# Attention heads: the two engines that subtract take strict turns, and two small jobs of a head move

## The reference, cut to what matters

```python
helical = jnp.einsum('bhpsc,bhptc->bhst', qn, kn) / p
dot = jnp.einsum('bshd,bthd->bhst', qh, kh) / math.sqrt(hd)
attn = jax.nn.softmax(alpha * dot + (1.0 - alpha) * helical, axis=-1)
vh = v.reshape(b, s, h, hd)
out = jnp.einsum('bhst,bthd->bshd', attn, vh).reshape(b, s, e)
```

## Time and profile before

| what | us |
|---|---|
| median of 3 runs (5803.75 to 5820.13) | 5806.87 |
| the profiled execution: its own time | 5804.25 |
| its span in the profile | 5802.5 |
| VectorE busy in the span | 4611.0 |
| TensorE busy | 3469.0 |
| ScalarE busy | 3017.1 |
| GpSimd busy | 2940.2 |

### The profile page before, as it was taken

One profiled execution on the slowest core, in us unless ns is written; L12 is line 12 of the kernel. 1 busy time (PEld: TensorE's weight loads), 2 busy tenths in 40 slices (PEclk: granted clock), 3 DMA queues, 4 the chain that ended last, 5 costly groups with the idle time before them and its releaser, 6 DMA issues. The chain is left out here.

```text
span 5802.5 us, 67231 instructions
## 1 busy us (share of the span) xinstructions
PE 3469.0 (60%) x14472; PEld 1229.5 (21%) x14472; DVE 4611.0 (79%) x8081; ACT 3017.1 (52%) x3827; POOL 2940.2 (51%) x2350
## 2 busy tenths in 40 slices
PE   8972000000000004878865799999999999999668
PEld 3330000000000002333411133333333333333123
DVE  5464686999999996553677799999999999999452
ACT  5563000001000013552287398989898989899632
POOL 1002465777777772112055266666666666666512
PEclk9986555555555557989987699999999999999888
DMA  1016415232322222000123311111111111110210
GB/s 40 15 36 112 74 16 111 58 65 49 65 53 61 64 50 62 13 11 0 68 101 121 65 32 32 43 36 32 32 33 32 32 32 32 33 44 6 78 27 29
DMA packets 143836, 275.46 MB, mean 47 GB/s; under 512 B 73808, under 2 KB 87504, under 8 KB 136336
## 3 DMA queue, kind: packets, MB, share of 16 engines
q1 hardware_dynamic: 142128, 263.57, 19.3%
q10 hardware_dynamic: 1440, 8.65, 0.4%
HBM read 178.65 MB, written 93.36 MB: 47 GB/s over the span
## 5 line engine op out<-in xcount | busy, mean ns | idle before, releaser
L994 POOL TENSOR_TENSOR att_heads_rest<-att_heads_probs,att_heads_high 128x576 f16<-128x576 f32 x1024 | 1390.4, 1358 | 848.8 <-ACT att_heads_high L1081 843.4
L1111 DVE TENSOR_REDUCE att_heads_maxima<-att_heads_peek 128x1 f32<-128x512 f32 x2048 | 1309.8, 679 | 91.8 <-PE att_heads_peek L1007 67.7
L1079 ACT ACTIVATE att_heads_probs<-att_heads_scores 128x1024 f32<-128x1024 f32 x1024 | 1074.4, 1049 | 252.3 <-PE att_heads_scores L1025 245.3
L1025 PE MATMUL att_heads_scores<-att_heads_q,att_heads_k 128*128 128x512 f16 (+1 forms) x4096 | 1067.2, 382 | 32.3 <-issue 21.5
L1081 ACT ACTIVATE att_heads_high<-att_heads_scores 128x1024 f16<-128x1024 f32 x1024 | 1075.8, 1051 | 0.0
L1849 PE MATMUL delta_out_sums<-delta_out_squares,main_head_sum 128*128 128x512 f32 x32 | 17.7, 688 | 1761.0 <-ACT delta_out_squares L1878 1761.0
L1131 DVE TENSOR_TENSOR att_heads_rest<-att_heads_probs,att_heads_high 128x448 f16<-128x448 f32 x1024 | 901.5, 881 | 63.8 <-POOL att_heads_rest L994 44.5
L1007 PE MATMUL att_heads_peek<-att_heads_k,att_heads_q 112*128 112x512 f16 x2048 | 688.9, 396 | 98.4 <-DVE att_heads_maxima L1111 49.3
L1728 ACT ACTIVATE delta_scan_s_terms<-delta_scan_state,delta_scan_record 128x64 f32<-128x64 f32 x256 | 104.7, 409 | 1160.2 <-DVE delta_scan_state L1785 1160.2
L1025 PEld LDWEIGHTS att_heads_scores<-att_heads_q,att_heads_k 128*128 128x128 f16 (+1 forms) x4096 | 395.5, 98 | 452.7 <-issue 37.2
L1041 PE MATMUL att_heads_out<-att_heads_high,att_heads_v_head 128*64 128x512 f16 x2048 | 418.5, 405 | 6.2 <-DVE att_heads_rest L1131 4.7
(11 more groups left out here) (225 smaller groups left out, 5393.9 us busy)
## 6 DMA issues: line engine op xcount, KB each, us to landing
delta_scan_record<-delta_record SPq DMA_DIRECT2D x64, 1026.0 KB, 10.6
att_heads_q<-att_hel SPq DMA_DIRECT2D x192, 128.0 KB, 3.1
att_heads_k<-att_hel SPq DMA_DIRECT2D x192, 128.0 KB, 3.2
delta_record<-delta_chunks_record SPq DMA_DIRECT2D x64, 256.5 KB, 4.7
att_hel<-att_hel_high SPq DMA_DIRECT2D x32, 512.0 KB, 3.8
att_hel<-att_hel_rest SPq DMA_DIRECT2D x32, 512.0 KB, 4.3
att_o<-att_heads_out_copy SPq DMA_DIRECT2D x256, 32.0 KB
att_out_parts<-att_o ACTq DMA_DIRECT2D x8, 1024.0 KB, 13.6
```

The costliest lines, as they stand in the source:

```text
L994: nc.gpsimd.tensor_tensor(rest[:, step % 4, SPLIT:], probs[:, step % 4, SPLIT:], high[:, step % 4, SPLIT:], ALU.subtract).then_inc(rest_b_ ...
L1025: mm = nc.tensor.matmul(scores[:, step % 2, tokens(j)], k[0:rows, slot, number, tile * P:(tile + 1) * P], q[0:rows, slot, number, tokens(h ...
L1079: nc.scalar.activation(probs[:, step % 4], scores[:, step % 2], ACT.Exp, scale=LOGIT_SCALE).then_inc(probs_ready, 1)
L1111: nc.vector.tensor_reduce(maxima[:, m:m + 1], peek[:, m % 2], AX.X, ALU.max).then_inc(peek_read, 1)
```

## The change

GpSimd waits, before its subtraction of a step, for VectorE's of the step before as well. VectorE's share of the columns goes from 448 to 480, GpSimd's from 576 to 544. `BEFORE_COPY` goes from 2 to 5. `LAST_PEEKS` goes from 23 to 22, so that `shifts` runs one step earlier while the transposition stays at step 24, and `shift_rows` goes from step 25, ahead of that step's maxima, to step 24, behind them.

```diff
-        BEFORE_COPY = 2
+        BEFORE_COPY = 5
         PEEKS = QT * 4
-        LAST_PEEKS = 23
+        LAST_PEEKS = 22
         EARLY = PEEKS - 2 * (LAST_PEEKS + 1)
-        TURN_AT = LAST_PEEKS + 1
-        ROWS_AT = TURN_AT + 1
+        TURN_AT = LAST_PEEKS + 2
         LOADS = 18 * 16
-        SPLIT = 448
+        SPLIT = 480
...
-            return 2, range(2 * (step - TURN_AT), 2 * (step - TURN_AT) + 2)
+            return 2, range(2 * (step - LAST_PEEKS - 1), 2 * (step - LAST_PEEKS - 1) + 2)
...
                             pool.wait_ge(high_ready, head * STEPS + step + 1 + H_CREDIT)
+                            pool.wait_ge(rest_a_ready, head * STEPS + step + R_CREDIT)
                             nc.gpsimd.tensor_tensor(rest[:, step % 4, SPLIT:], probs[:, step % 4, SPLIT:], high[:, step % 4, SPLIT:],
                                                     ALU.subtract).then_inc(rest_b_ready, 1)
...
                         by, numbers = peeks_at(step)
-                        if step == ROWS_AT and exists(last, slot, 1):
-                            shift_rows(*later(quad, slot, 1))
                         if exists(last, slot, by):
                             read_peeks(*later(quad, slot, by), numbers)
+                        if step == TURN_AT and exists(last, slot, 1):
+                            shift_rows(*later(quad, slot, 1))
                         if step == LAST_PEEKS and exists(last, slot, 1):
                             shifts(*later(quad, slot, 1))
```

## The result

| | us |
|---|---|
| before, median of 10 runs (5803.75 to 5820.13) | 5810.09 |
| with the change, median of 10 runs (5825.05 to 5844.25) | 5836.27 |
| ratio, with its 95% interval | 1.0041 (1.0032 to 1.0050) |
| span of the profiled execution with the change | 5835.6 |

The change makes the kernel 26 us slower, and the interval leaves out no change.

What follows compares the result with a forecast made beforehand. GpSimd's and VectorE's alternating subtractions were taken to bound every step of the heads' stage: 1023 x 2.115 us plus extras gave 2209.8 against 2185.3, +24.5 us, so 5830 in all, range 5786 to 5865.

Steps and rivals of the forecast that it cites:

- The four terms: Each step: GpSimd's subtraction, handing to VectorE, VectorE's subtraction, handing back, in series; 2.115 us.
- GpSimd's start behind VectorE: Fourth term, from VectorE's end to GpSimd's start: 0.14 us, with 0.09 as the lower end.
- the rival: Short handing over from VectorE to GpSimd, if a satisfied first semaphore costs nothing: 0.09 us, about 5779; 15 in 100.
- the copy: GpSimd's copy of values between two subtractions, once a head: ends 0.33 us late, 10.2 us in all.
- The turn of the loop: TensorE issues nothing for 3.65 us, 7 times; 4.9 us each reach the chain, 34.3 in all.
- The two more maxima: Two more maxima before the first step: 1.2 us.
- the entry of the loop: Entry of the first loop, put at 0.5 us.
- BEFORE_COPY: Takes away ScalarE's wait for the last `weigh` of a half; costed at nothing, as ScalarE has time free.
- The shifts: LAST_PEEKS 22 and moved `shift_rows` take away TensorE's wait for reduced maxima; no effect, lying in idle time.
- The rule of the port: Shared port as exclusive lock: 283 us of blocked time disappear, 137 us less in the stage, 5670; 3 in 100.

Runs made afterwards that it cites:

- e3_gpsimd_one: The changed kernel, with GpSimd's subtraction waiting for VectorE's semaphore only, the wait for high taken by the instruction ahead; 5774.23 us.
- e7_copy2: e4_both_one with BEFORE_COPY back from 5 to 2; 5713.13 us.
- e8_shifts_back: The changed kernel with the shifts put back (LAST_PEEKS 23, shift_rows at step 25 ahead of the maxima); 5856.89 us.
- e4_both_one: e3_gpsimd_one, with VectorE's subtraction too waiting for one semaphore only, GpSimd's; 5709.88 us.
- e6_one_no_turns: e4_both_one without GpSimd's wait for VectorE's subtraction of the step before; 5828.30 us.
- e2_no_wait: The changed kernel without GpSimd's new wait, keeping the 480 and 544 columns and the moved copies and shifts; 5811.36 us.
- e1_wait_only: The kernel before with GpSimd's new wait alone, its columns, copies and shifts as they were; 5877.12 us.

## Why the prediction was right

*The four terms.* Predicted 1.215 + 0.10 + 0.66 + 0.14 = 2.115; read off after, 1.216, 0.10, 0.66 and 0.14, and a step of 2.12. The one term without a row of its own, GpSimd's start behind VectorE, was taken from L1744, an instruction with two semaphores, and not from L860 with one. That choice had the sign in it: with L860's 0.09 the forecast would have been 5779, and `e3_gpsimd_one`, where the gap is 0.08, measured 5774. Here the rival's price was right and its condition was not met.

*From the step to the stage.* Predicted 24.5 us more, measured 22.3 from first to last subtraction. Two errors met. At 2.12 rather than 2.115 the steps give about 8 us more. All that is not step was put at 34.3 + 10.2 + 1.2 + 0.5 = 46.2 us. Measured, it is what is left of the stage: the median distance of two starts in the whole list is 2.123, and 2207.6 - 1023 x 2.123 = 35.8, so 10 less. That the two errors nearly cancel is luck. By terms: the copy costs 0.26 a head and not 0.33, so 8.1 for 10.2. The turn of the loop was counted 7 times and stops TensorE 6 times; it holds 17.7 at the four steps behind it, 2.9 a turn where I gave 4.9, and another 7.2 at the step ahead of a group of four heads, where GpSimd pauses, which the prediction does not have: 24.9 for 34.3. The two more maxima (1.2) stand ahead of the first subtraction, so they are no part of this sum, and the first step took 2.12, so nothing for the entry of the loop. One slip is in the last line as well: 5828.8 + 2.6 is 5831.4, and not 5830.

*Costed at nothing.* `BEFORE_COPY`: right (`e7_copy2`). The shifts: as a part of the change, right in the sum, since the new order has no such wait. But the reason was incomplete. I said that both parts shorten waits of engines that have time to spare. `e8_shifts_back` shows that TensorE has too little to spare for this one under the turns: the wait reaches VectorE and costs 14 us at its own place, and 21 by the medians.

*The rule of the port.* The rows had a second engine standing still, and the Trainium skill (SBUF — State Buffer, Who interferes with whom) calls the shared port pair an exclusive lock. The trace agrees as far as it goes: with the turns no subtraction of either kind is stretched in the middle of a half, and in the last head before the change GpSimd's ends 1.14 us behind VectorE's where it takes 1.28 alone, so all but 0.14 of it comes after VectorE's end. That the port is the cause, and not something else that the two share, no run here tests. But VectorE's stalls fell from 283 us to (666 - 647) x 1024 = 19, and that was not 264 us less of time. They came back as waiting, as forecast, because the handing over twice a step is dearer than standing in the queue: in the last head the step is 1.86 us in contention and 2.12 in turns.

## What to carry to other kernels

When two engines get in each other's way, putting them in turns makes a chain in series: add up both durations and both handings over before calling it a gain. Each handing over is short, but it is paid at every step, and the number of semaphores on the waiting instruction is part of its price. Take the wait that is fulfilled first off the instruction that stands on the chain, and give it to the one ahead of it; then the same turns that lost 26 us here gain 100. Look in the trace whether that has worked everywhere: here it had not in the four heads behind VectorE's loop.

## What the runs showed of the hardware that was not expected

- An instruction that waits for two semaphores, where the last to come is the one that the code names last, starts later than with one: on GpSimd 0.145 us instead of 0.079 behind VectorE's end, on VectorE 0.103 instead of 0.034 behind GpSimd's (medians of the changed kernel, `e3_gpsimd_one` and `e4_both_one`). The other order of the two was not run. The first I had from the trace of before; that VectorE's own handing over shrinks by as much was an inference until it ran.
- GpSimd's subtraction stretches from 1.22 to 1.66 us when it starts 0.07 us behind VectorE's (`e6_one_no_turns`). Where that happens the step is short, 1.956 us in the median, against 2.150 in the other steps, where as a rule VectorE is the one stretched.
- Where the loop over four heads turns, VectorE pauses for 1.5 us ahead of its second subtraction, beside TensorE's 3.6. It does so without the turns too (9.7 us in 6 pauses in `e2_no_wait`). GpSimd's pause of 1.5 us ahead of its copy of the values is in the traces where its subtraction waits for two semaphores (the changed kernel, `e1_wait_only`, `e8_shifts_back`), and in none of the others; why is open.
